# Cross-attention and expert-choice FFN on one core: token lists of the last five experts written to DRAM by indirect transfers, and two DMA transposes queued ahead of weight loads

## What is computed

```python
x = x + _L0_xattn_ref(_layernorm(x), ctx_768, Wq, Wk, Wv, Wo, bo)
# the FFN, on _layernorm(x):
k = int(EXPERT_CAPACITY * t / e)                      # 512 tokens for each expert and batch
probs = jax.nn.softmax(jnp.einsum('ntd,ed->nte', x, gate_w), axis=-1)
g, m = jax.lax.top_k(probs.transpose(0, 2, 1), k)     # gates and token numbers
xin = x[batch_idx, m]
h = jax.nn.gelu(jnp.einsum('nekd,edf->nekf', xin, w1), approximate=False)
h = jnp.einsum('nekf,efd->nekd', h, w2)
out = zeros.at[batch_idx, m].add(g[..., None] * h)    # added to x
```

## Time and profile before

| | |
|---|---|
| median of 3 runs | 1667.96 us (1666.43 to 1668.12) |
| the profiled execution's own time | 1667.86 us |
| its span in the trace | 1665.7 us |
| PE busy | 1647.2 us (99%) |
| DVE, ACT, POOL busy | 1103.0, 942.7, 304.3 us (66%, 57%, 18%) |
| mean granted TensorE clock | 0.996 |
| share of the 16 DMA engines: SP's queue, POOL's queue | 25.9%, 10.7% |

### The profile page before, as it was taken

The page is one execution under the profiler, slowest core; times in us unless marked ns, Lnnn a source line. Parts: engine busy times, 40 slices in busy tenths (PEclk is TensorE's granted clock), DMA queues, the critical chain, the costliest instruction groups (busy, mean ns, idle before and its releaser), DMA issues.

```text
span 1665.7 us, 23177 instructions
## 1 busy us (share of the span) xinstructions
PE 1647.2 (99%) x8508; PEld 1407.7 (85%) x8508; DVE 1103.0 (66%) x1992; ACT 942.7 (57%) x2045; POOL 304.3 (18%) x364
## 2 busy tenths in 40 slices
PE   9999999999999999999999999999999999999997
PEld 9999999877888887888888888888888888888886
DVE  7555697877766648655775576558655855686663
ACT  5678777744332556456646654666466546654441
POOL 3233233111122110300140023003300320040002
PEclk9999999999999999999999999999999999999999
DMA  3243436354334473512451244234423432342004
GB/s 134 77 142 111 152 128 222 120 152 127 127 77 164 129 176 111 129 26 76 135 118 26 77 141 111 46 88 120 101 76 90 96 93 77 101 96 57 26 1 51
DMA packets 134917, 171.06 MB, mean 103 GB/s; under 512 B 62701, under 2 KB 63881, under 8 KB 134809
## 3 DMA queue, kind: packets, MB, share of 16 engines
q1 hardware_dynamic: 120441, 136.04, 25.9%
q0 software_dynamic: 14336, 33.56, 10.7%
q10 hardware_dynamic: 32, 0.03, 0.0%
HBM read 121.38 MB, written 33.55 MB: 93 GB/s over the span
## 4 chain that ended last, share of the span: by engine, by line
PE 94%; DMA 2%; ACT 2%; DVE 1%; issue 0%; POOL 0%; POOLq 0%; SPq 0%; ACTq 0%; DVEq 0%
PE ps L2218 10%; PE ps L2216 10%; PE ps L2217 10%; PE ps L2196 9%; PE ps L2195 9%; PE ps L2194 9%; PE ps L1229 4%; PE ps L1230 4%; PE ps L1231 4%; PE ps L2131 3%; PE ps L2118 3%; PE ps L2120 3%; PE ps L2119 3%; PE ps L2132 3%; PE ps L2133 3%; DMA turned_planes<-planes 1%
## 5 line engine op out<-in xcount | busy, mean ns | idle before, releaser
L2216 PE MATMUL ps<-v2h,hhS 128*128 128x512 f32 x768 | 298.8, 389 | 0.0
L2218 PE MATMUL ps<-v2h,hlS 128*128 128x512 f32 x768 | 298.8, 389 | 0.0
L2217 PE MATMUL ps<-v2l,hhS 128*128 128x512 f32 x768 | 298.8, 389 | 0.0
L2195 PE MATMUL ps<-Tl,Wh 128*128 128x512 f32 x672 | 261.4, 389 | 0.0
L2196 PE MATMUL ps<-Th,Wl 128*128 128x512 f32 x672 | 261.4, 389 | 0.0
L2194 PE MATMUL ps<-Th,Wh 128*128 128x512 f32 x672 | 261.4, 389 | 0.0
L1598 POOL DMA_INDIRECT out_dram<-YS,tok_idx x48 | 105.0, 2187 | 816.2 <-DVE YS L2027 805.0
L2027 DVE SCALAR_TENSOR_TENSOR YS<-ps,tok_gate,YS 128x512 f32<-128x512 f32 x144 | 106.4, 748 | 120.0 <-PE ps L2218 120.0
L1771 ACT ACTIVATE v2h<-w_raw 128x512 fp32r<-128x512 f32 x96 | 57.4, 622 | 215.7 <-PE ps L2218 215.7
L2217 PEld LDWEIGHTS ps<-v2l,hhS 128*128 128x128 f32 x768 | 144.2, 188 | 30.0
L2216 PEld LDWEIGHTS ps<-v2h,hhS 128*128 128x128 f32 x768 | 144.2, 188 | 29.9
(11 more groups left out here) (284 smaller groups left out, 3599.2 us busy)
## 6 DMA issues: line engine op xcount, KB each, us to landing
w_raw<-in_L_ffn_w_dram SPq DMA_DIRECT2D x80, 1024.0 KB, 7.2
XB<-in_x_dram SPq DMA_DIRECT2D x16, 512.0 KB, 4.1
XR<-in_x_dram SPq DMA_DIRECT2D x16, 512.0 KB, 6.3
out_dram<-X SPq DMA_DIRECT2D x16, 512.0 KB, 5.0
xn_rows<-XN SPq DMA_DIRECT2D x16, 512.0 KB, 5.3
w_raw<-in_L_xattn_Wq_dram SPq DMA_DIRECT2D x1, 1024.0 KB, 9.1
wo_sb<-in_L_xattn_Wo_dram SPq DMA_DIRECT2D x2, 512.0 KB, 11.5
w_raw<-in_L_xattn_Wk_dram SPq DMA_DIRECT2D x1, 768.0 KB, 6.0
```

Source lines behind the costliest of these rows:

```text
L2195: nc.tensor.matmul(ps[:, bank, :], wh, tl, start=False, stop=False, **go_on)
L2216: nc.tensor.matmul(ps[:, bank, :], th, wh, start=(t == 0), stop=False)
L2217: nc.tensor.matmul(ps[:, bank, :], th, wl, start=False, stop=False)
L2218: last = nc.tensor.matmul(ps[:, bank, :], tl, wh, start=False, stop=(t == GF - 1))
```

## The change

Of the 16 lookups the first six stay: those of `PLAIN` and of expert 2 (`LX = 1`). For experts 3 to 7 of each batch (ten lists) the tokens go by DRAM instead. DVE computes for every token where its entry goes in a list (`list_at`): at its rank if it is chosen, else at 512 plus its own number, behind the part that is read. POOL writes the token numbers with `iota` and DVE the gates into `pairs` (number and gate, 8 bytes a token). POOL then issues for each list 16 indirect transfers of 128 pairs, 160 in all, between its gathers and scatters, waits for all of them, and reads the first 512 entries of each list into `tok_pair` with ten plain transfers. `gather_pair`, `scatter_pair` and `evict` take token and gate from `tok_pair` for x of 1 and more. `pairs` lies where `Wh` is written from slot 61 on, so ACT waits there for all list transfers.

Also: SP issues the transposes of x = 0 ahead of the loads of weight groups 14 and 15; chunk 0 of a turned `PLAIN` expert moves from slot 13 to slot 14; `dve_vals` covers three experts of a batch in place of eight; and two semaphores are merged into a third (`s_T1`, `s_T2` into `s_Td`), with the same waits.

```diff
-        CONSTS = 16
+        CONSTS = 17
+            pool.iota(away[:], pattern=[[P, NT]], base=CAP, channel_multiplier=1,
+                      allow_small_or_imprecise_dtypes=True).then_inc(c_const, 1)
...
+        NPE, LX = 2, 1
+        away = fixed("away", [P, NT])
+        tok_pair = fixed("tok_pair", [P, COLS, CT, 2], U32)
+        list_at = fixed("list_at", [P, B, E - NPE - LX, NT], U32)
+        pairs = put("pairs", 59392, [P, B, E - NPE - LX, NT, 2], U32)
...
+        def dve_list_places(dve, b):
+
+            shape = [P, E - NPE - LX, NT]
+            far = away[:].unsqueeze(1).broadcast_to(shape)
+            link(nc.vector.tensor_tensor(q1[:, NPE + LX:E], place[:, NPE + LX:E], far, ALU.subtract))
+            link(nc.vector.tensor_tensor(q2[:, NPE + LX:E], q1[:, NPE + LX:E], chosen[:, NPE + LX:E], ALU.mult))
+            nc.vector.tensor_tensor(list_at[:, b], q2[:, NPE + LX:E], far, ALU.add).then_inc(v_list, 1)
+
+        def dve_pairs(dve, b):
+
+            nc.vector.tensor_copy(pairs[:, b, :, :, 1].bitcast(F32), probs[:, b, NPE + LX:E, :]).then_inc(v_list, 1)
+
         def dve_rows(dve, b):
 
+            dve_list_places(dve, b)
+            dve.wait_ge(v_list, 2 * b + 1)
...
-        NPE = len(PLAIN) // B
-        LOOKUPS = PLAIN + tuple(b * E + e for e in range(NPE, E) for b in range(B))
+
+        LOOKUPS = PLAIN + tuple(b * E + e for e in range(NPE, NPE + LX) for b in range(B))
+        d_list, d_tok, v_list = (sem(n) for n in "d_list d_tok v_list".split())
+
+        LISTS = tuple((b, x) for b in range(B) for x in range(E - NPE - LX))
...
                 if at(i, CHOICE + 2):
-                    dve_vals(0, 1, E // 2)
+                    dve_vals(0, 1, NPE + LX)
...
-        SPLIT_AT, WORDS_AT, CHUNKS_AT = (10, 11), (12, 13), {13: (0,), 14: (1,), 15: (2, 3)}
+        SPLIT_AT, WORDS_AT, CHUNKS_AT = (10, 11), (12, 13), {14: (0, 1), 15: (2, 3)}
...
             for gg in range(2, G * len(PLAIN)):
+                if gg >= 4 * G - 2:
+                    for a in range(2):
+                        sp_turn(sp, (0, 4 * G - 1 - gg), a)
                 sp_weights(sp, gg)
                 if gg in (G, 3 * G):
                     for a in range(2):
                         sp_turn(sp, (gg // G,) if gg == G else (3,), a)
-                if gg >= 4 * G - 2:
-                    for a in range(2):
-                        sp_turn(sp, (0, 4 * G - 1 - gg), a)
...
+            def token_at(x, c, q):
+                return tok_idx[:, c, q:q + 1] if x < LX else tok_pair[:, c, q, 0:1]
+
+            def write_lists(first, last):
+                for m in range(first, last):
+                    b, x = LISTS[m]
+                    if x == 0:
+                        pool.wait_ge(v_list, 2 * (b + 1))
+                        pool.wait_ge(c_const, CONSTS + B)
+                    for t in range(NT):
+                        pool.indirect_dma_start(out=lists[b * E + NPE + LX + x],
+                                                out_offset=bass.IndirectOffsetOnAxis(ap=list_at[:, b, x, t:t + 1], axis=0),
+                                                in_=pairs[:, b, x, t, :], in_offset=None).then_inc(d_list, 16)
+
+            def read_lists(x):
+                pool.wait_ge(d_list, 16 * NT * len(LISTS))
+                for b in range(B):
+                    c = b * E + NPE + LX + x
+                    pool.dma_start(tok_pair[:, c], lists[c][0:CAP, :].rearrange("(p q) v -> p q v", p=P)).then_inc(d_tok, 16)
+
             def gather_pair(x, b):
                 c = b * E + NPE + x
-                pool.wait_ge(h_idx, LOOKUPS.index(c) + 1)
+                if x < LX:
+                    pool.wait_ge(h_idx, LOOKUPS.index(c) + 1)
+                else:
+                    pool.wait_ge(d_tok, 16 * len(LISTS))
...
-            for i in range(len(PLAIN) - 1):
-                pool_gather(pool, i + 1)
-                if i == len(PLAIN) - 2:
-                    gather_pair(0, 1)
-                    gather_pair(0, 0)
-                scatter(i)
+            for b in range(B):
+                pool.iota(pairs[:, b, :, :, 0], pattern=[[0, E - NPE - LX], [P, NT]], base=b * S,
+                          channel_multiplier=1).then_inc(c_const, 1)
+            write_lists(0, 1)
+            pool_gather(pool, 1)
+            write_lists(1, 3)
+            scatter(0)
+            write_lists(3, 4)
+            pool_gather(pool, 2)
+            write_lists(4, 6)
+            scatter(1)
+            pool_gather(pool, 3)
+            gather_pair(0, 1)
+            write_lists(6, 9)
+            gather_pair(0, 0)
+            scatter(2)
+            write_lists(9, 10)
+            for x in range(E - NPE - LX):
+                read_lists(x)
             scatter(len(PLAIN) - 1)
...
                 if n == T_AT + 5:
+                    act.wait_ge(d_list, 16 * NT * len(LISTS))
                     for idx in W_ORDER[0:3]:
                         w_high(0, idx)
...
-                if n == 2:
-                    dve_vals(0, E // 2, E - 2)
-                if n == KF + 1:
-                    dve_vals(0, E - 2, E)
+                if n == 0:
+                    dve_pairs(dve, 0)
...
                 if n == VALS_AT:
-                    dve_vals(1, 0, E)
+                    dve_vals(1, 0, NPE + LX)
+                    dve_pairs(dve, 1)
...
-                gate = tok_gate[:, j // CT * E + NPE + x, j % CT:j % CT + 1]
+                c, q = j // CT * E + NPE + x, j % CT
+                gate = tok_gate[:, c, q:q + 1] if x < LX else tok_pair[:, c, q, 1:2].bitcast(F32)
+                if x == LX and g == 0 and j == 0:
+                    dve.wait_ge(d_tok, 16 * len(LISTS))
```

More of the change, by code:

```diff
@@ L43, in xattn_expert_choice @@
     xn2_rows = nc.dram_tensor("xn2_rows", (B * S, D), F32, kind="Internal").ap()
+    lists = [nc.dram_tensor(f"list{c}", (CAP + S, 2), U32, kind="Internal").ap() for c in range(COLS)]
     x_blk = x.rearrange("b (n t p) d -> (b n) p t d", t=TPB, p=P)
@@ L1491, in xattn_expert_choice @@
         s_raw2 = [sem(f"s_raw2_{i}") for i in range(2)]
-        (s_prod, s_u1, s_c11, s_u2, s_u7, s_c22, s_c21, s_gelu, s_hid, s_sum, s_Wh, s_Wl, s_v2h, s_v2l, s_dn, s_ev, s_Ta, s_Tb, s_T1,
-         s_T2, s_Td, s_Th, s_Tl, s_scat) = (sem(f"s_{n}") for n in (
-             "prod u1 c11 u2 u7 c22 c21 gelu hid sum Wh Wl v2h v2l dn ev Ta Tb T1 T2 Td Th Tl scat").split())
+        (s_prod, s_u1, s_c11, s_u2, s_u7, s_c22, s_c21, s_gelu, s_hid, s_sum, s_Wh, s_Wl, s_v2h, s_v2l, s_dn, s_ev, s_Ta, s_Tb,
+         s_Td, s_Th, s_Tl, s_scat) = (sem(f"s_{n}") for n in (
+             "prod u1 c11 u2 u7 c22 c21 gelu hid sum Wh Wl v2h v2l dn ev Ta Tb Td Th Tl scat").split())
         s_rows = [sem(f"s_rows{b}") for b in range(B)]
@@ L1582, in gather_pair @@
                     pool.wait_ge(s_Tb, 3 * x)
-                    pool.wait_ge(s_Td, x)
+                    pool.wait_ge(s_Td, 3 * x)
                 elif b == 0:
@@ L1587, in gather_pair @@
                     pool.indirect_dma_start(out=rows_in[b][:, q, :], out_offset=None, in_=xn2_rows,
-                                            in_offset=bass.IndirectOffsetOnAxis(ap=tok_idx[:, c, q:q + 1], axis=0),
+                                            in_offset=bass.IndirectOffsetOnAxis(ap=token_at(x, c, q), axis=0),
                                             ).then_inc(s_rows[b], 16)
@@ L1598, in scatter_pair @@
                 pool.indirect_dma_start(out=out_rows,
-                                        out_offset=bass.IndirectOffsetOnAxis(ap=tok_idx[:, c, q:q + 1], axis=0),
+                                        out_offset=bass.IndirectOffsetOnAxis(ap=token_at(x, c, q), axis=0),
                                         in_=YS[:, j, :], in_offset=None, compute_op=ALU.add,
@@ L1743, in t_high @@
                     if idx == TT3:
-                        act.wait_ge(s_T1, x + 1)
+                        act.wait_ge(s_Td, 3 * x + 1)
                     elif idx == TT2:
-                        act.wait_ge(s_T2, x + 1)
+                        act.wait_ge(s_Td, 3 * x + 2)
                     elif idx == TT4:
-                        act.wait_ge(s_Td, x + 1)
+                        act.wait_ge(s_Td, 3 * (x + 1))
                     nc.scalar.activation(Th[:, idx], Tf[:, idx], ACT.Copy).then_inc(s_Th, 1)
@@ L1944, in t_sum @@
                 elif idx == TT1:
-                    nc.vector.tensor_tensor(Tf[:, TT1], x1, x0, ALU.subtract).then_inc(s_T1, 1)
+                    nc.vector.tensor_tensor(Tf[:, TT1], x1, x0, ALU.subtract).then_inc(s_Td, 1)
                 elif idx == TT2:
-                    dve.wait_ge(s_T1, x + 1)
-                    nc.vector.tensor_tensor(Tf[:, TT2], x1b, Tf[:, TT1], ALU.subtract).then_inc(s_T2, 1)
+                    dve.wait_ge(s_Td, 3 * x + 1)
+                    nc.vector.tensor_tensor(Tf[:, TT2], x1b, Tf[:, TT1], ALU.subtract).then_inc(s_Td, 1)
                 else:
-                    dve.wait_ge(s_T2, x + 1)
```

(1 more changed line is left out.)

## The result

The changed kernel takes 1656.36 us (median of 4 runs, 1654.47 to 1658.91) beside 1667.79 for the kernel before (4 runs, 1666.43 to 1668.12): ratio 0.9938, 95% interval 0.9922 to 0.9954, so 11.4 us less. The profiled run took 1658.91 us, 8.95 less than the profiled run of before; the forecast was 12.9. The kernel is faster: by 1.5 us less than the sum in the medians, by 4.0 less in the profiled run, which is the slowest of the four.

A forecast was written before the change was run, and what follows sets the result against it. PE, busy 1647.2 of 1665.7 us, was taken to bound the kernel. Lookups 5.5, transposes ahead of weights 6.5 and chunk 0.9 sum to 12.9 us off 1667.86, so 1655.0 us; range 1653.0 to 1662.5.

The forecast's parts named there:

- The sum: Whole kernel: 5.5 + 6.5 + 0.9 = 12.9 us off the profiled 1667.86, giving 1655.0 us.
- Lookups: PE in the slots: ten lookups removed at 0.55 us each save 5.5 us, 4.2 at the least.
- Transposes ahead of weights: SP's queue for batch 0, slots 53 and 54: PE's whole gap goes, 6.5 us; bounds 0 to 6.5.
- POOL's work is hidden: cost 0: List transfers and ten reads on POOL meet every deadline, so they cost PE 0 us.
- the gap stays: Rival: transposes stay slow beside list writes and scatters, or group 14 is late; 6.4 us gained, 1661.5 us; chance 0.09.
- new small gaps: Rival: 160 more transfers disturb DVE, or some ACT wait gets through; 3 to 8 us back, 1658 to 1663; chance 0.08.
- The chunk: Slot 13: with chunk 0 in slot 14, PE no longer waits for late counts; 0.9 us saved, bounds 0 and 0.9.
- List writes: POOL's indirect 8-byte-pair transfers: 1.35 us from start to start, like a gather; bounds 1.24 and 2.37.
- The list's dates: POOL's schedule: gather 1 ends at 352, gather 2 keeps 442.33, pair (0,0) lands at 588, not needed before 596.
- What is late next: Slot 52: ACT's own work, 6.2 us against a 5.4 us slot; at worst batch 1's side or weight group 14.
- Slow rival: Rival: list writes too slow on POOL, kernel slower than before from 1.64 us each; 1710 us at 1.92; chance 0.09.
- Signs: Expected traces: no lookup matmul behind 480 us, no idle PE at slot 54's end, clock 1.00, transposes landing in 4 to 5 us.

The follow-up runs named there:

- the floor: Slots length without PE's gap, 355.87 us, taken from the changed kernel with all list transfers and their reads left out; that kernel's median is 1654.36 us.
- before's second execution: The unchanged kernel profiled once more with no edit: slots 367.67 us, time 1666.02 us in 1 run.
- after: The changed kernel itself, with the whole change, beside the unchanged kernel: median 1656.36 us, ratio 0.9938.

## Why the prediction was right

1655.0 was forecast and 1656.36 measured, inside the range. The mechanism is right in its three terms; what the forecast left out is a new gap, worth 4.0 us in the profiled execution and less in most others. Step by step:

- **The sum.** Slots of before less the floor: 368.67 - 355.87 = 12.8, forecast 12.9. Four kernels reach it, the changed one doesn't. From before's second execution it would be 11.8: the 2.9 us of slow clock in the sum came from one execution, and part of that is chance.
- **Lookups, 5.5.** The new order alone gives 362.19; from there to the floor are 6.3 us, of which 0.9 are the chunk, so 5.4 for ten, 0.54 each. Right. Taking the distance between down matmul and up matmul, less the matmuls between, was the right reading. The small bound (4.2) was the distance to the next matmul alone.
- **Transposes ahead of weights, 6.5.** 6.5 in the kernel before. The gap that the prediction priced is gone in the changed kernel as well, and ACT finds batch 0's halves there without a wait. (It stood at the end of slot 56; the prediction looks for it at the end of slot 54.) All the same this is **the term that was mis-sized** in the changed kernel: "I take the whole gap as gone" puts nothing on the transposes of batch 1, though the prediction says itself that the wait may move "to batch 1's side". A gap opened there that cost 4.0 us in the profiled execution and 2.0 in the second. The landing time of 4.3 us was read without lists. In the kernels with lists the transposes of `PLAIN[3]` took 6 to 13 us to land, and batch 1's 11.9 and 15.6. Also, "the 5.2 us that it may be late" was batch 0's slack; batch 1's is some 8 us, which kept the gap small.
- **"POOL's work is hidden: cost 0".** Every deadline of POOL was met, and the work cost 2 to 4 us all the same, since I had regard to when POOL's transfers end, and not to whose transfers they run beside. The rival "the gap stays" had named the cause (list writes and scatters at the same time) with 0.09, and "new small gaps" had the size with 0.08: a few us of ACT's wait get through, 3 to 8 us back. The profiled execution has that rival's 4.0; that the median is only 1.4 above the forecast is in part luck, since the size of the gap varies between executions.
- **The chunk, 0.9.** 1.15 to 0.23 by the rows. In the kernel with the chunk alone the count of slot 14 comes without a wait as well (387.94, the matmul before it at 387.71).
- **List writes.** Forecast 1.35 us from start to start, measured 1.069 + 0.30 = 1.37. The gather was the right neighbour, not the scatter. The overlapping rows hold also against the 2.0 us that the Trainium skill fits to each such transfer ("DMA: Bandwidth & Descriptors", "Anatomy of one DMA"): 160 transfers followed one another at 1.37 us. The 2 us for each write beside a one-hot were too much by a little (2.59, 2.52 and 2.28 us, where an undisturbed one takes 0.96).
- **The list's dates.** Gather 1 was to end at 352, starts at 347.35 and ends at 352.5; gather 2 keeps 441.75; pair (0,0) was to have landed by 588, is issued from 577.04 to 581.9 and lands by 586.0. Right to 2 us.
- **Reads.** 5.5 us for ten where 12 to 20 were allowed. Nothing hangs on it.
- **What is late next.** Weight group 14 was named and is late by 2.22 us in after, behind transposes that took 13.76. By the forecast's own figure of at most 13.0 it would just have had room: its second load is issued at 598.96, and ACT asks at 613.1. It took 16.3 us to land, so the bound of 13.0, read without lists, was too small as well. PE doesn't stand for it a second time.
- **Slow rival.** Its threshold was 1.64 us a write at 160 writes; 200 writes at 1.37 are worth 1.71 and are slower than before, as it says. Its place, ACT's split of slot 52's rows, is right.
- **Signs.** Two signs of being right did not come: transposes landing in 4 to 5 us, and a clock of 1.00 throughout the slots. The others did: the last lookup matmul starts at 475.1, list writes take 0.96 us undisturbed, the groups keep 0.227 us a matmul, and ACT waits for neither gathered rows nor lists in the slots named.

## What to carry to other kernels

When transfers are moved into an idle stretch of one engine, list the latency-bound transfers of the other queues in the same stretch, and price those at the slowest row seen beside similar traffic, not at the median. Many small transfers count here as well: the 8-byte writes made transposes and weight loads land later where they were compared, near 363 and 543 us, and where the scatters came on top this used up the slack that had hidden it. Order within one queue is worth as much as the work saved: here 6.5 us for a few lines, and without it the lists gave back all the 5.4 of the lookups. A small edit that beats the changed kernel in the traces is to let the accumulating scatter wait until the transposes have landed (or the last list, with the same 355.9 us of slots): 355.84 us of slots against 357.9 and 359.9, median 1654.29 against 1656.66 on the same chip, though the two intervals (0.9915 to 0.9942 and 0.9938 to 0.9965) just overlap.

## What the hardware showed that was not expected

- Batch 1's pair of transposes keeps SP's queue for 5.4 us with neither scatter 2 nor list 9 beside it, and with list 9 alone; for 6.8, 9.3 and 11.9 us with the four accumulating scatters (three kernels), and for 10.4 and 13.8 where 16 indirect writes follow the scatters. The three kernels differ in how far the scatters are ahead: the first is issued 7.0, 6.6 and 1.7 us before the transposes. That orders the three numbers, but the step from 6.8 to 9.3 is too large for the 0.4 us between them, and its cause is open.
- Indirect writes of 128 times 8 bytes, without any scatter or gather beside them, make transposes land later: near 543 us they take 6.0 to 13.4 us where they take 4.3 to 4.6 without the writes, and a 1 MB weight load next to them takes 14.6 and 16.9 us (two kernels) where it takes 8.2. How much of the first comes by way of the second is open.
- An indirect write of 128 times 8 bytes takes POOL as long as an indirect gather of 128 rows of 2 KB: 0.96 us against 0.94 to 1.00 in the rows above and the earlier trace rows, 0.30 us apart. The bytes don't count there.
- The gap at the end of slot 56 measured 6.5 and 5.5 us in two executions of the kernel before, and 4.5 and 2.2 with ten lookups fewer. Idle times of 1.8 and 1.9 us left the clock at 1.00 and cost 2.0 and 2.2; idle times of 2.2 to 3.5 us were followed by a stretch at 0.50 and cost 4.0 to 6.5. A gap is not a fixed price.
